# Cross-attention with its key products in the output's PSUM banks and no drain on ScalarE

## The reference, cut to what matters

```python
q = (layernorm(x) @ wq).reshape(1, 128, 16, 64)      # 128 queries
k = (ctx @ wk).reshape(1, 12544, 16, 64)             # 12544 keys
v = (ctx @ wv).reshape(1, 12544, 16, 16)
attn = softmax(q @ k.T / sqrt(64))                   # per head
x = x + (attn @ v)                                   # heads side by side, 256 features
# then: windowed self-attention, gated feed-forward, a second cross-attention over the
# same context, a causal self-attention, and a mixture of 16 experts (2 per query)
```

## Time and profile before

| what | value |
| --- | --- |
| median of three runs | 977.97 us |
| the profiled execution | 978.08 us |
| its span, first to last instruction | 976.3 us |
| TensorE busy | 944.2 us, 97% |
| VectorE busy | 707.8 us, 72% |
| ScalarE busy | 587.4 us, 60% |
| GpSimd busy | 411.2 us, 42% |
| granted TensorE clock, mean | 0.996 |

### The profile page before, as it was taken

How to read it: one execution, slowest core, us unless ns; L and a number is a source line. 1 busy time by engine, 2 the same in 40 slices (tenths; PEclk the granted TensorE clock), 3 DMA queues, 4 the chain that set the end, 5 groups by cost and what they waited for, 6 DMA issues and landing times.

```text
span 976.3 us, 31089 instructions
## 1 busy us (share of the span) xinstructions
PE 944.2 (97%) x13321; PEld 709.1 (73%) x13321; DVE 707.8 (72%) x900; ACT 587.4 (60%) x1404; POOL 411.2 (42%) x478
## 2 busy tenths in 40 slices
PE   6999999999999999999999999988989999999998
PEld 5666666666666666666666666667978877889998
DVE  3788888888888888888888888865025654467886
ACT  5676666666676666666667666642236664336664
POOL 2454455544555554554454544430113331513332
PEclk9999999999999999999999999999999999999999
DMA  6010001000000000000000100019938999408992
GB/s 232 24 25 25 25 24 25 24 24 25 24 24 24 25 24 24 11 17 25 24 24 24 25 24 3 4 58 405 301 127 265 284 274 311 173 2 286 322 338 96
DMA packets 78551, 98.07 MB, mean 100 GB/s; under 512 B 21584, under 2 KB 56928, under 8 KB 78432
## 3 DMA queue, kind: packets, MB, share of 16 engines
q1 hardware_dynamic: 77344, 94.67, 30.3%
q10 hardware_dynamic: 1088, 1.57, 0.4%
HBM read 95.68 MB, written 0.13 MB: 98 GB/s over the span
## 4 chain that ended last, share of the span: by engine, by line
PE 68%; ACT 11%; DVE 10%; issue 4%; ACTq 3%; POOL 2%; DMA 1%; DVEq 0%; SPq 0%; POOLq 0%
PE ps L352 29%; PE ps L394 10%; PE ps L361 7%; PE ps L1591 6%; ACT probs L572 6%; DVE x_peak L667 5%; PE ps L404 4%; ACTq L583 3%; PE ps L1067 3%; PE ps L1608 2%; PE ps L1612 2%; PE ps L1609 2%; ACT x_pr L1233 1%; DVE c1T_lo L1271 1%; DVE x_negc L1277 1%
## 5 line engine op out<-in xcount | busy, mean ns | idle before, releaser
L572 ACT ACTIVATE probs<-ps,x_peak 128x512 f32<-128x512 f32 (+1 forms) x400 | 269.7, 678 | 173.8 <-DVE x_peak L667 155.3
L667 DVE TENSOR_REDUCE x_peak<-ps 128x2 f32<-128x1024 f32 (+1 forms) x200 | 240.4, 1204 | 58.5 <-PE ps L394 56.2
L686 DVE STREAM_TRANSPOSE probsT<-probs 128x1024 f32<-128x1024 f32 (+1 forms) x200 | 225.6, 1182 | 3.5 <-ACT probs L572 3.5
L394 PE MATMUL ps<-keys,qT 64*32 64x512 f32 (+1 forms) x3200 | 223.2, 584 | 1.3 <-ACT keys L559 0.8
L860 POOL TENSOR_SCALAR vals<-vals_t,x_side 128x512 f32<-128x512 f32 (+1 forms) x100 | 152.8, 1540 | 122.3 <-PEq L412 122.3
L352 PE MATMUL ps<-ctxT_hi,wk_hi 128*128 128x512 f32 (+1 forms) x400 | 165.3, 413 | 5.7 <-ACTq L583 4.8
L404 PEld LDWEIGHTS ps<-probsT,vals 64*32 64x32 f32 x6144 | 112.8, 106 | 72.3 <-issue 71.8
L352 PE MATMUL ps<-ctxT_lo,wk_hi 128*128 128x512 f32 (+1 forms) x400 | 155.5, 389 | 0.0
L352 PE MATMUL ps<-ctxT_hi,wk_lo 128*128 128x512 f32 (+1 forms) x400 | 155.3, 388 | 0.0
L559 ACT COPY keys<-ps 128x512 f32<-128x512 f32 (+1 forms) x200 | 115.3, 577 | 35.8 <-PE ps L352 30.4
L352 PEld LDWEIGHTS ps<-ctxT_hi,wk_hi 128*128 128x128 f32 x400 | 75.3, 188 | 78.5 <-ACTq L583 46.5
(11 more groups left out here) (255 smaller groups left out, 1322.7 us busy)
## 6 DMA issues: line engine op xcount, KB each, us to landing
m_w<-in_m_w SPq DMA_DIRECT2D x32, 1024.0 KB, 7.6
ctx_raw<-in_ctxT SPq DMA_DIRECT2D x24, 512.0 KB, 4.1
ctx_two<-in_ctxT SPq DMA_DIRECT2D x24, 512.0 KB, 4.2
ctx_one<-in_ctx SPq DMA_DIRECT2D x24, 512.0 KB, 5.3
x_shrinkT<-x_shrink SPq DMA_DIRECT2D x384, 1.0 KB, 1.7
f_h1T<-in_f_h1T SPq DMA_DIRECT2D x1, 4096.0 KB, 18.1
f_h2T<-in_f_h2T SPq DMA_DIRECT2D x1, 4096.0 KB, 27.8
m_shared_w<-in_m_sw SPq DMA_DIRECT2D x2, 1024.0 KB, 7.8
```

What stands on the lines that cost most here:

```text
L394: i = pe.matmul(m.ps[32 * j:32 * (j + 1), SCORE_BANKS[t % HALF] + odd, 0:nt * P], m.qT[rows, 4 * group + j, qs], m.keys[rows, 4 * group + ...
L572: return act.activation(m.probs[t % HALF][:, odd, 0:nt * P], m.ps[:, SCORE_BANKS[t % HALF] + odd, 0:nt * P], ACT.Exp, bias=m.peak[slot][:, ...
L667: dv.tensor_reduce(m.peak[slot][:, 1, cs, t % HALF], m.ps[:, bank:bank + 2, 0:nt * P], AX.X, ALU.min).then_inc(s["dve" if t == STEPS - 1 e ...
L686: i = dv.transpose(m.probsT[slot][:, cs, 0:4 * nt, t % HALF * 32:t % HALF * 32 + 32], m.probs[t % HALF][:, :, 0:nt * P].rearrange("p c (b ...
```

## The change

The drain and its semaphore `scores_read` go; TensorE waits for `probs_ready` instead, which the second exponential of a step raises. Key groups are always in banks 4 and 5, where the weighted output is. They therefore wait for `turn_out`. The weighted output of a unit has two pieces of 48 and 80 matmuls, after score steps 0 and 1. VectorE does `turn_out` between the second and the third maximum. VectorE's hardware loop over pairs of chunks is unrolled.

```diff
-KEY_BANK, FIRST_BANK, VALUE_BANK, OUT_BANK = 2, 4, 6, 4
+KEY_BANK, VALUE_BANK, OUT_BANK = 4, 6, 4
...
     def wide(slot, first_pair, half, nt):
 
-        pe.wait_ge(s["scores_read"], n("scores_read"))
+        output_turned()
         for q in range(HALF):
-            if q == 2:
-                output_turned()
             if q >= 2:
                 pe.wait_ge(s["k_kept"], n("k_kept"))
             key_group(slot, first_pair + q, nt)
-        pe.wait_ge(s["scores_read"], n("scores_read"))
+        pe.wait_ge(s["probs_ready"], n("probs_ready", 2))
         value_group(slot, half, nt)
...
         pe.wait_ge(s["k_kept"], n("k_kept", 2))
-        pe.wait_ge(s["scores_read"], n("scores_read"))
+        pe.wait_ge(s["probs_ready"], n("probs_ready"))
         of = range(2 * nt_before * half, 2 * nt_before * (half + 1))
-        cuts = (0, 3 * len(of) // 8, 6 * len(of) // 8, len(of))
+        cut = 3 * len(of) // 8
...
-            weighted(1 - slot, of[cuts[t]:cuts[t + 1]], of)
-        pe.wait_ge(s["scores_read"], n("scores_read"))
+            if t < 2:
+                weighted(1 - slot, of[cut:] if t else of[:cut], of)
+        pe.wait_ge(s["probs_ready"], n("probs_ready"))
         scores(HALF * half + 3, nt)
...
         exponential(slot, t, 1, nt).then_inc(s["probs_ready"], 1)
-        act.drain().then_inc(s["scores_read"], 1)
...
-        for t in range(first, first + HALF):
+        for t in range(first, first + 2):
             maxima(slot, t, CHUNK_TILES)
         if half == 1 or order >= 2:
             dv.wait_ge(s["acc_added"], n("acc_added"))
         turn_out()
+        for t in range(first + 2, first + HALF):
+            maxima(slot, t, CHUNK_TILES)
...
-    looped = ("scores_full", "dve", "probs_ready", "v_full", "out_full", "acc_added", "rescaled")
-    n.restart(dv, s, *looped)
-    with dv.Fori(0, (N_FULL - 2) // 2):
+    for _ in range((N_FULL - 2) // 2):
         chunk(0, 2)
         chunk(1, 2)
-        n.restart(dv, s, *looped)
```

More of the change, by code:

```diff
@@ L455, in first_chunk @@
                 pe.wait_ge(s["k_kept"], n("k_kept"))
-            key_group(0, p, nt, FIRST_BANK)
+            key_group(0, p, nt)
         pe.wait_ge(s["q_ready"], n("q_ready"))
@@ L474, in first_chunk @@
             pe.wait_ge(s["k_kept"], n("k_kept"))
-            value_group(0, half, nt, FIRST_BANK + half)
-        pe.wait_ge(s["scores_read"], n("scores_read", 3))
+            value_group(0, half, nt, KEY_BANK + half)
+        pe.wait_ge(s["probs_ready"], n("probs_ready", 3))
         for t in (4, 5):
@@ L482, in first_chunk @@
         for p in (0, 1):
-            key_group(1, p, CHUNK_TILES, FIRST_BANK)
+            key_group(1, p, CHUNK_TILES)
         scores(6, nt)
-        pe.wait_ge(s["scores_read"], n("scores_read"))
+        pe.wait_ge(s["probs_ready"], n("probs_ready"))
         scores(7, nt)
@@ L488, in first_chunk @@
             pe.wait_ge(s["k_kept"], n("k_kept"))
-            key_group(1, p, CHUNK_TILES, FIRST_BANK)
-        pe.wait_ge(s["scores_read"], n("scores_read", 2))
+            key_group(1, p, CHUNK_TILES)
+        pe.wait_ge(s["probs_ready"], n("probs_ready", 2))
         value_group(1, 0, CHUNK_TILES)
@@ L615, in first_chunk @@
             split_key_weights(half)
-        keep_keys(0, nt, FIRST_BANK)
+        keep_keys(0, nt)
         keep_queries(0)
         for p in (1, 2, 3):
-            keep_keys(p, nt, FIRST_BANK)
+            keep_keys(p, nt)
         act.wait_ge(s["wv"], 16)
@@ L634, in first_chunk @@
         for p in (0, 1):
-            keep_keys(p, CHUNK_TILES, FIRST_BANK)
+            keep_keys(p, CHUNK_TILES)
         exponentials(0, 6, nt)
-        keep_keys(2, CHUNK_TILES, FIRST_BANK)
+        keep_keys(2, CHUNK_TILES)
         exponentials(0, 7, nt)
@@ L640, in first_chunk @@
         split_context(0, 0, CHUNK_TILES)
-        keep_keys(3, CHUNK_TILES, FIRST_BANK)
+        keep_keys(3, CHUNK_TILES)
     first_chunk(TAIL_TILES)
@@ L742, in first_chunk @@
         for half in range(2):
-            turn_values(0, half, nt, FIRST_BANK + half)
+            turn_values(0, half, nt, KEY_BANK + half)
         for t in (4, 5):
```

## The result

The changed kernel takes 979.34 us (median of 20 runs, 977.74 to 983.28); before, 20 runs of the same comparison have a median of 976.77 us (975.14 to 978.86). The ratio is 1.0032, 95% interval 1.0023 to 1.0042: slower by 0.3%, about 3 us. The forecast was 978.8, range 975.0 to 982.5, with no measurable change as the likeliest case (0.48) and slower at 0.35. The time is inside the range and the cycle came out as worked out; the likeliest case was not the one that came. As a change, the forecast was +0.8 us on a median of 977.97, and about +3 us on 976.77 was measured: the closeness of 979.34 to 978.8 is partly that of the reference, which lay 1.2 us lower in the longer comparison.

The account below looks back on a forecast made before the run. A cycle through TensorE, ScalarE and VectorE was taken to bound the kernel. Units +2.0, pauses +0.4, start -1.06 and -0.4, end -0.3 gave +0.6 us on 978.08: 978.7, stated as 978.8, range 975.0 to 982.5.

Parts of the forecast that it names:

- no measurable change: Whole kernel: balance as computed, 976.0 to 979.9 us, a difference under 0.2% from before; chance 0.48.
- slower: Whole kernel: longer second weighted piece (0.32) and falling clock (0.02), together with leftovers; chance 0.35.
- the cycle: One unit through TensorE, ScalarE and VectorE: 12.91 us instead of 12.77 or 12.85; +2.0 us over 45 units.
- The drain's gain lost in ScalarE's wait for maximum 2: ScalarE, step 2: the drain's 0.20 us per step is lost waiting for maximum 2, which allows exponentials only at 5.92.
- Turning, bank and loop at nothing: VectorE's 0.37 us turning hidden before maximum 2, key group's new wait free by itself, removing loop returns worth 0.
- The pauses: TensorE ahead of step 3's last matmul, eight of 45 units: maximum 3's slack leaves 0.4 us of 1.9.
- the slower rival: Longer second weighted piece decides: units of 12.96, all 1.9 us of pauses kept, 3.8 us higher, 982.5; chance 0.32.
- The end: Last unit: transposes of probabilities start right behind the maxima without 0.37 us of turning between; -0.3 us.
- The start: Second chunk's two units near 12.25 instead of 12.78, -1.06 us; first chunk's drains on the chain, -0.4 us.

## Why the prediction was right, and where it was not

- **The cycle** was right to 0.03 us at the stations on the path: step 2 at 3.48 (3.49), maximum 2 at 4.66 (4.66), copy at 7.96 (7.93), third key group at 8.59 (8.57), unit 12.91 (12.89). The first key group is later than I wrote (5.40, not 5.2), which is hidden by the wait behind it: I had counted 0.86 us for step 3, but it is 1.05 from its start to a key group that waits for nothing. By the same number the wait there before was about 0.16 us, not 0.34.
- **The drain's gain lost in ScalarE's wait for maximum 2** was right, and is shown from both sides: with three pieces 13 us faster than before, with the drain in the changed kernel only 0.17 to 0.20 us a unit slower.
- **Turning, bank and loop at nothing** was right: the turning is covered by 0.34 us, the loop measured as 1.0001, and bank and place of the turning together make no difference to a quiet unit's length.
- **The pauses** were the term that failed: I kept 0.4 us of 1.9 and they cost 5.5. The step in words: I argued that pauses ahead of step 3's last matmul would be absorbed, and took their places as given. The first half holds in the main (0.8 us are left of them), the second does not. The edge that in the kernel before fell on the 16th matmul of the third weighted piece, behind step 2 (it is 160 matmuls into the unit in both), where no unit showed a pause of this size, falls to the end of the second piece in the changed kernel, ahead of step 2 and straight on the new path. I had named this as part of the slower rival ("any pause there moves maximum 2"), which I priced at 982.5 and put at 0.32. Of its two parts the pauses came, 5.1 us above my sum instead of 1.5, and the longer quiet unit of 12.96 did not.
- **The end** was mis-sized: 0.3 us for 2.2. I counted the turning on VectorE and missed who waits for it there, the 5.22 us of weighted matmuls.
- **The start**: two units at 12.08 instead of 12.25, -1.4 for -1.06. The first chunk was 2.1 us shorter for 0.4, but 1.3 of it is the first load of weights (5.59 instead of 6.39 us) and the first key groups (3.06 instead of 3.58), and these vary between kernels that do the same work there: the fifth score step starts at 25.45 before, at 24.67 with VectorE's loop written out and at 23.71 with 32 instructions more, where the changed kernel has 23.61. The other 0.8 can be the drains, for which I had 0.4; no run separates them.

That the time hit so well is in part luck: the two large misses, pauses 5.1 us too low and the end 1.9 us too high, have opposite signs. With the 1.3 us of the start left out, the two profiled executions differ by 0.9 + 1.3 = 2.2 us. The medians say 2.6 and the ratio 3.1, and the pauses differ from one execution to the next, so about 1 us stays unassigned.

## What to carry to other kernels

Write the cycle as offsets from one point for every engine and look for the two longest chains into the same instruction: taking 0.20 us a step off one of them was worth nothing here where the same edit lengthened the other, and 1.3% without that. An edit that only moves code past a place where an engine pauses changes the time as much as its dependencies do, so before a difference of 0.5% is ascribed to an order of work, shift the code by a few instructions and measure again. The faster versions here keep the old order and drop the drain; with the last unit turned early they take 962.7 us, and with 16 instructions in front 961.4, which the intervals do not separate.

## What the runs showed of the hardware

Pauses of TensorE that no semaphore explains (its weight loads idle for 0.3 to 1.35 us) lie a multiple of 256 of its instructions apart: they followed shifts of 16 and 32 instructions exactly, by 8 and 16 matmuls. Most edges cost nothing. The two of every seven that did end stretches of small matmuls, where the roughly 128 loads and 128 matmuls since the edge before took about 2.5 and 3.3 us (an estimate from the timelines of the changed kernel), against 10 us and more where key groups lie between them. A short stretch is not enough, though: by the same count a third edge, 2.9 us into the other unit of half 1, ends one of about 2.9 us, and no pause was seen there. The Trainium skill (Runtime: NRT & Kernel Launch, Instruction fetch mechanics) says that instructions come in blocks of 16 KiB, 256 instructions, and that crossing an edge is mostly hidden. This trace agrees on the size (16,384 bytes a packet); on the cost it shows 5.5 us in 45 units of the changed kernel, and 10.4 us more in them by a shift of 32 instructions (595.98 against 585.54). Whether a pause is a wait for the packet itself, why the third edge shows none, and why the same edge pauses in some chunks and not in others, was not settled.
